# A lane shuffle, merged stack loads, held-back and column-tiled projections in the opening of an attention kernel

## The reference

```python
q, k, v = (x @ W + b for W, b in ((Wq, bq), (Wk, bk), (Wv, bv)))   # split in 16 heads of 16
q = q * cos + rotate_half_interleaved(q) * sin                      # pairs (-x1, x0)
k = k * cos + rotate_half_interleaved(k) * sin
x = layernorm(x + softmax(q @ k.T / sqrt(16)) @ v)
x_prev = x shifted by one token (zero first)
xr, xk = mu_r * x + (1 - mu_r) * x_prev, mu_k * x + (1 - mu_k) * x_prev
out = layernorm(x + sigmoid(xr @ W_r.T) * (relu(xk @ W_k.T) ** 2 @ W_v.T))
```

## Time and profile before

| | |
|---|---|
| time, median of 3 runs | 1582.94 us (1581.42 to 1584.07) |
| profiled execution, its own time | 1584.12 us |
| its span, first to last instruction | 1582.3 us |
| TensorE, VectorE, ScalarE, GpSimd busy | 98%, 85%, 72%, 21% |
| mean granted TensorE clock | 0.993 |

### The profile page before, as it was taken

How to read it: one execution, slowest core, us unless ns; L and a number is a source line. 1 busy time by engine, 2 the same in 40 slices (tenths; PEclk the granted TensorE clock), 3 DMA queues, 4 the chain that set the end, 5 groups by cost and what they waited for, 6 DMA issues and landing times. The chain is left out here.

```text
span 1582.3 us, 47773 instructions
## 1 busy us (share of the span) xinstructions
PE 1545.5 (98%) x21184; PEld 765.5 (48%) x21184; DVE 1345.3 (85%) x1398; ACT 1139.0 (72%) x2187; POOL 335.3 (21%) x327
## 2 busy tenths in 40 slices
PE   5999999999999999999999999999999999999997
PEld 3343445555445544455445444544444455443574
DVE  3447999999999999999999999999999999996577
ACT  3225777777777777777777777777777777778442
POOL 2330322112221322132213221121210000001165
PEclk9999999999999999999999999999999999999999
DMA  6625211121101111121112111211101111000012
GB/s 230 182 73 174 76 22 22 22 76 19 18 15 45 48 22 22 22 75 22 23 22 75 22 22 22 75 22 18 19 16 17 22 22 22 3 2 2 1 41 67
DMA packets 34735, 68.20 MB, mean 43 GB/s; under 512 B 9760, under 2 KB 19744, under 8 KB 32736
## 3 DMA queue, kind: packets, MB, share of 16 engines
q1 hardware_dynamic: 32560, 62.03, 16.0%
q10 hardware_dynamic: 1968, 3.12, 0.5%
HBM read 26.97 MB, written 11.53 MB: 24 GB/s over the span
## 5 line engine op out<-in xcount | busy, mean ns | idle before, releaser
L931 DVE TENSOR_REDUCE tile_max<-ring_ps 128x1 f32<-128x1024 f32 x1024 | 1204.2, 1216 | 164.6 <-PE ring_ps L446 163.5
L696 ACT ACTIVATE probs<-score_ps 128x512 f32<-128x512 f32 x2048 | 1059.6, 603 | 270.6 <-PE score_ps L543 270.1
L446 PE MATMUL ring_ps<-k_stack,q_stack 96*32 96x512 bf16 x8192 | 838.9, 381 | 11.0 <-DMA q_stack<-rope 10.1
L543 PE MATMUL score_ps<-q_stack,k_stack 99*32 99x512 bf16 x8192 | 841.7, 381 | 4.0 <-ACT probs L696 2.9
L479 PE MATMUL pv_ps<-probs,v_aug 128*32 128x512 f32 x4096 | 541.5, 592 | 0.0
L543 PEld LDWEIGHTS score_ps<-q_stack,k_stack 99*32 99x32 bf16 x8192 | 258.8, 96 | 311.7 <-ACT probs L696 146.8
L446 PEld LDWEIGHTS ring_ps<-k_stack,q_stack 96*32 96x32 bf16 x8192 | 253.5, 96 | 309.0 <-DVE tile_max L931 120.5
L479 PEld LDWEIGHTS pv_ps<-probs,v_aug 128*32 128x32 f32 x4096 | 146.7, 111 | 82.7 <-ACT probs L696 1.6
L773 POOL TENSOR_TENSOR neg_cuts<-neg_max,zeros 128x16 bf16<-128x16 f32 x32 | 7.0, 220 | 740.5 <-DVE neg_max L918 740.5
L766 POOL TENSOR_TENSOR v_aug<-v_all,b_v_s 128x256 f32<-128x256 f32 x32 | 23.3, 730 | 281.5 <-PE pv_ps L479 256.1
L425 PE MATMUL score_ps<-xz,w_qk_s 128*128 128x512 f32 x96 | 50.8, 657 | 6.4 <-DMA b_qk_s<-b_qk 6.4
(11 more groups left out here) (73 smaller groups left out, 544.6 us busy)
## 6 DMA issues: line engine op xcount, KB each, us to landing
q_stack<-rope SPq DMA_DIRECT2D x186, 64.0 KB, 2.4
k_stack<-rope SPq DMA_DIRECT2D x186, 64.0 KB, 2.4
qk_raw<-probs SPq DMA_DIRECT2D x28, 256.0 KB, 2.5
rope<-qk_raw SPq DMA_DIRECT2D x7, 1024.0 KB, 4.8
rope<-qk_raw SPq DMA_DIRECT2D x14, 512.0 KB, 6.9
xz<-x_ch SPq DMA_DIRECT2D x8, 512.0 KB, 6.7
xz<-x_tok SPq DMA_DIRECT2D x2, 2048.0 KB, 12.9
out<-xz SPq DMA_DIRECT2D x8, 512.0 KB, 2.9
```

What stands on the lines that cost most here:

```text
L446: mm = pe.matmul(ring_ps[k % 2][g:g + VCOLS, c * TOK:(c + 1) * TOK], q_stack[0:ROWS, buf, qt * P + g:qt * P + g + VCOLS], k_stack[0:ROWS, ...
L543: mm = pe.matmul(score_ps[n % SCORE_BANKS][g:g + VCOLS, :], k_stack[0:ROWS_M, h % STACKS, kt * P + g:kt * P + g + VCOLS], queries[:, j], s ...
L696: act.activation(probs[:, kt % 2, j, :], score_ps[n % SCORE_BANKS][:, :], ACT.Exp, scale=SCALE).then_inc(exps_done, 1)
L931: dve.reduce_max(tile_max[:, h % 2, unit // 2, unit % 2:unit % 2 + 1], slot[:, :], AX.X)\
```

## The change

- Quad 0 is taken out of PSUM by VectorE instead of ScalarE, in blocks of 512 columns: `stream_shuffle` exchanges neighbouring partitions, `scalar_tensor_tensor` adds the bias and multiplies by cosine or sine (`turn_block`). The swap DMAs go; the bias table has a fifth column with the exchanged biases. All cuts of quad 0 go by blocks of 512 (`block_of(n)`).
- A head's stacks are loaded by six DMAs: a query part is repeated over its bands in one transfer, and key parts 0 to reps - 1 go together.
- The x blocks of batch 1 are issued after head 0's stack loads. SyncE issues two stack loads behind each store.
- Batch 1's values are projected last instead of after its first quad. Five projections are held back and follow later entries of `OPENING` (`HELD_BACK`).
- Each projection matmul with 128-wide weights becomes four with 32-wide weights, to four column groups.
- `evacuated` counts from projection 4 on, so all waits on it are lower by 4; the new semaphore `quad0_taken` frees the first four banks.

```diff
@@ -25,9 +25,9 @@
-BANDS = [(a, c) for a in range(PARTS) for c in range(PARTS - a)]
-LOADS = 2 * len(BANDS)
-ROWS = len(BANDS) * HEAD_DIM
+BAND_GROUPS = [(a, PARTS - a) for a in range(PARTS)]
+LOADS = 2 * PARTS
+ROWS = sum(reps for _, reps in BAND_GROUPS) * HEAD_DIM
@@ -60,9 +60,11 @@
         yield from (("qk", first, n) for n in range(BLOCKS))
-        yield from (("v", b, n) for n in range(TILES // 2))
-        for g in range(first + 1, first + QUADS // BATCH):
-            yield from (("qk", g, n) for n in range(BLOCKS))
+        if b == 0:
+            yield from (("v", b, n) for n in range(TILES // 2))
+        yield from (("qk", g, n) for g in range(first + 1, first + QUADS // BATCH) for n in range(BLOCKS))
+        if b > 0:
+            yield from (("v", b, n) for n in range(TILES // 2))
@@ -89,6 +91,7 @@
+HELD_BACK = {("max", 0, MAX_UNITS - 1): 1, ("max", 1, 1): 1, ("neg", 0, 0): 1, ("max", 1, 2): 1, ("max", 1, 3): 1}
@@ -295,25 +302,21 @@
-            def swap(n):
-
-                sp.wait_ge(evacuated, n + 1)
-                t = slice(n * TOK, (n + 1) * TOK)
-                for e in range(2):
-                    sp.dma_start(swapped[e::2, t], raw[1 - e::2, t]).then_inc(swap_in[n // 2], DMA)
-
             def load_part(h, part, t):
 
                 buf, side, row = h % STACKS, h // QUAD % 2, h % QUAD * HEAD_DIM
-                for band, (a, c) in enumerate(BANDS):
-                    rows = slice(band * HEAD_DIM, (band + 1) * HEAD_DIM)
+                q = cuts[row:row + HEAD_DIM, side, :, t]
+                k = cuts[QUAD_ROWS + row:QUAD_ROWS + row + HEAD_DIM, side, :, t]
+                first = 0
+                for a, reps in BAND_GROUPS:
+                    rows = slice(first * HEAD_DIM, (first + reps) * HEAD_DIM)
+                    first += reps
                     if a == part:
-                        sp.dma_start(q_stack[rows, buf, t], cuts[row:row + HEAD_DIM, side, a, t])\
+                        sp.dma_start(q_stack[rows, buf, t], q[:, a:a + 1, :].broadcast_to([HEAD_DIM, reps, t.stop - t.start]))\
                             .then_inc(stack_in[buf], DMA)
                         yield
-                    if c == part:
-                        sp.dma_start(k_stack[rows, buf, t], cuts[QUAD_ROWS + row:QUAD_ROWS + row + HEAD_DIM, side, c, t])\
-                            .then_inc(stack_in[buf], DMA)
+                    if reps - 1 == part:
+                        sp.dma_start(k_stack[rows, buf, t], k[:, 0:reps, :]).then_inc(stack_in[buf], DMA)
                         yield
@@ -352,29 +355,23 @@
             for n in range(BLOCKS):
                 load_x(n)
-            swap(0)
-            swap(1)
-            load_x(BLOCKS)
-            load_x(BLOCKS + 1)
-            swap(2)
-            swap(3)
-            load_x(BLOCKS + 2)
-            load_x(BLOCKS + 3)
             for i in range(2):
                 for part, signal in enumerate((high_ready, mid_ready, low_ready)):
-                    sp.wait_ge(signal, i + 1)
+                    sp.wait_ge(signal, 2 * (i + 1))
                     for _ in load_part(0, part, half_of(i)):
                         pass
+            for n in range(BLOCKS, A_GROUPS):
+                load_x(n)
...
-                    for _ in range(3):
+                    for _ in range(2):
                         next(others, None)
@@ -409,7 +409,10 @@
-                after(pe, evacuated, n - len(proj_ps) + 1)
+                if n >= 2 * len(proj_ps):
+                    pe.wait_ge(evacuated, n - len(proj_ps) - BLOCKS + 1)
+                elif n >= len(proj_ps):
+                    pe.wait_ge(quad0_taken, n - len(proj_ps) + 1)
@@ -422,8 +422,9 @@
                     for c in range(CHUNKS):
-                        mm = pe.matmul(bank[:, :], w_qk_s[:, c, m:m + P], x_s[:, b, c, t:t + TOK],
-                                       start=c == 0, stop=c == CHUNKS - 1)
+                        for r in range(0, P, VCOLS):
+                            mm = pe.matmul(bank[r:r + VCOLS, :], w_qk_s[:, c, m + r:m + r + VCOLS],
+                                           x_s[:, b, c, t:t + TOK], start=c == 0, stop=c == CHUNKS - 1)
@@ -431,8 +432,10 @@
                         for c in range(CHUNKS):
-                            mm = pe.matmul(bank[:, k * DIM:(k + 1) * DIM], x_s[:, a, c, t:t + P], w_v_s[:, c, :],
-                                           start=c == 0, stop=c == CHUNKS - 1, skip_group_check=True)
+                            for r in range(0, P, VCOLS):
+                                mm = pe.matmul(bank[r:r + VCOLS, k * DIM:(k + 1) * DIM],
+                                               x_s[:, a, c, t + r:t + r + VCOLS], w_v_s[:, c, :],
+                                               start=c == 0, stop=c == CHUNKS - 1, skip_group_check=True)
@@ -573,10 +576,11 @@
-                if n < len(WORK):
+                if op in HELD_BACK or n + sum(HELD_BACK.values()) < len(WORK):
                     project(n)
                     n += 1
@@ -652,33 +656,35 @@
+            cut_high(0)
+            cut_high(1)
+            cut_mid(0)
+            take(BLOCKS)
+            cut_high(2)
+            cut_mid(1)
+            take(BLOCKS + 1)
+            cut_high(3)
+            cut_mid(2)
+            take(BLOCKS + 2)
+            cut_mid(3)
+            for n in range(BLOCKS + 3, len(WORK)):
                 take(n)
@@ -879,36 +885,48 @@
-            def turn_half(i):
-
-                t = half_of(i)
-                dve.wait_ge(tables_in[i], 2 * DMA)
-                dve.wait_ge(swap_in[i], 4 * DMA)
-                dve.wait_ge(evacuated, 2 * (i + 1))
-                dve.tensor_tensor(raw[:, t], raw[:, t], cos_s[:, t], ALU.mult)
-                dve.tensor_tensor(swapped[:, t], swapped[:, t], sin_s[:, t], ALU.mult).then_inc(products, 1)
-                dve.wait_ge(products, i + 1)
+            def turn_block(n):
+
+                t, bank = block_of(n), proj_ps[n]
+                dve.wait_ge(projected, n + 1)
+                dve.stream_shuffle(swapped[:, t], bank[:, :], [lane ^ 1 for lane in range(32)]).then_inc(swap_ready, 1)
+                if n == 0:
+                    dve.wait_ge(w_first_in, 2 * DMA)
+                dve.wait_ge(tables_in[n // 2], 2 * DMA)
+                dve.scalar_tensor_tensor(raw[:, t], bank[:, :], b_qk_s[:, 0:1], cos_s[:, t], ALU.add, ALU.mult)\
+                    .then_inc(quad0_taken, 1)
+                dve.wait_ge(swap_ready, n + 1)
+                dve.scalar_tensor_tensor(swapped[:, t], swapped[:, t], b_qk_s[:, QUADS // BATCH:], sin_s[:, t],
+                                         ALU.add, ALU.mult).then_inc(products, 1)
+                dve.wait_ge(quad0_taken, n + 1)
+                dve.wait_ge(products, n + 1)
                 dve.tensor_tensor(raw[:, t], raw[:, t], swapped[:, t], ALU.add).then_inc(rot_ready, 1)
...
-            turn_half(0)
+            turn_block(0)
+            turn_block(1)
             cut_rest(0)
-            turn_half(1)
+            turn_block(2)
+            cut_rest(1)
             cut_low(0)
-            cut_rest(1)
             cut_low(1)
+            turn_block(3)
+            cut_rest(2)
+            cut_rest(3)
+            cut_low(2)
+            cut_low(3)
```

More of the change, by code:

```diff
@@ L146, in build @@
         w_v_s = sb("w_v_s", [P, CHUNKS, DIM])
-        b_qk_s = sb("b_qk_s", [P, QUADS // BATCH])
+        b_qk_s = sb("b_qk_s", [P, QUADS // BATCH + 1])
         b_v_s = sb("b_v_s", [P, DIM])
@@ L217, in build @@
         stage_out = [sem(f"stage_out{i}") for i in range(STAGES)]
-        swap_in = [sem(f"swap_in{i}") for i in range(2)]
+        quad0_taken = sem("quad0_taken")
+        swap_ready = sem("swap_ready")
         raw_in = sem("raw_in")
@@ L280, in half_of, with block_of @@
             return slice(i * HALF, (i + 1) * HALF)
+        def block_of(n):
+            return slice(n * TOK, (n + 1) * TOK)
         def z_tile(tile):
@@ L326, in store_raw @@
                 s = STORED[g, t]
-                sp.wait_ge(evacuated, n + 1)
+                sp.wait_ge(evacuated, n - BLOCKS + 1)
                 sp.dma_start(raw_d[g, :, t * TOK:(t + 1) * TOK], stage[:, s % STAGES, :])\
@@ L336, in load_raw @@
                 if g == 1:
-                    sp.wait_ge(low_ready, 2)
+                    sp.wait_ge(low_ready, BLOCKS)
                 else:
@@ L376, in _ @@
             load_neg(0)
-            sp.wait_ge(evacuated, len(WORK))
+            sp.wait_ge(evacuated, len(WORK) - BLOCKS)
             for b in range(BATCH):
@@ L575, in _ @@
                     pass
-                if n < len(WORK):
+                if op in HELD_BACK or n + sum(HELD_BACK.values()) < len(WORK):
                     project(n)
                     n += 1
-            pe.wait_ge(evacuated, len(WORK))
+            assert n == len(WORK)
+            pe.wait_ge(evacuated, len(WORK) - BLOCKS)
             for h in range(ALL_HEADS):
@@ L654, in take, with cut_high, cut_mid @@
```

(49 more changed lines are left out.)

## The result

| | before | changed |
|---|---|---|
| median | 1583.12 us (1581.42 to 1584.07, 4 runs) | 1558.83 us (1558.47 to 1560.27, 4 runs) |
| ratio, 95% interval | | 0.9847 [0.9832, 0.9863] |
| profiled execution, span | 1584.12, 1582.3 | 1558.66, 1556.9 |

A forecast was written before the change was run, and what follows sets the result against it. TensorE, busy for all 42.0 of 42 us, was taken to bound the attention, so only its start moves: 8.4 + 16.2 + 0.2 = 24.8 us off the 1582.94 median gives 1558.1, range 1553 to 1570.

The forecast's parts named there:

- First maximum, 8.4 us: Opening: TensorE's first maximum begins at 32.2 us instead of 40.6, 8.4 us earlier.
- the two paths: Opening, before the first maximum: stack loads complete at 31.1 us, TensorE's projections 7 to 11 end at 31.6.
- Turn and stretch, 16.2 us: First maximum to first score: turns of 2.155 us instead of 2.46, stretch 78.7 instead of 94.9, 16.2 less.
- First scores, 0.2 us: First score to first probabilities-by-values product: 5.2 us instead of 5.40, held by VectorE's reading, 0.2 less.
- Attention and epilogue unchanged: After the way into the attention: nothing that runs there is touched, so times stay equal to the end.
- The sum: Whole kernel: 8.4 + 16.2 + 0.2 = 24.8 us saved, giving 1558.1; own range 1556 to 1561, chance 0.46.
- Rival A: Turns stay at 2.46 us if the bf16 to f32 change costs the 0.31: 11.2 us kept, 1569.3; chance 0.14.
- F: Projections: 107 ns is the floor of an f32 pair, value projections take 3.44 us, time 1580; chance 0.03.
- C: Projections: narrow tiles' weight loads stay exposed, 110 ns each, 58 us in the turns, time 1616; chance 0.03.
- the estimate from the 60 cycles a matmul: Projections: 12 or 24 added pairs at 25 ns cost 0.3 or 0.6 us each; sum 13 us smaller in turns.
- D: Opening: slow shuffle or late transfers put the first maximum at 34 to 36, 1560 to 1562; with B 0.20.
- B: Clock falls in the 2.8 us gap or first scores, costing 2 to 4 us: 1560 to 1562; with D 0.20.

The follow-up runs named there:

- the last kernel: The changed kernel with the gap filled (projections 4 to 7 in the idle ring banks, 13 before the first maximum) and a sixth projection held back: 1557.24 us, ratio 0.9837.

## Why the prediction was right, point by point

*First maximum, 8.4 us: right, 8.40.* That it is met so closely is partly luck: the two paths were worked out to end at 31.1 and 31.6, 32.2 was chosen above both, and they end at 31.8 (the last load, 29.48 + 2.3) and 32.24; the second profile has 32.75. The last low cut was forecast to end at 27.8 and ends at 27.97; the shuffle takes 0.73 us for the 0.70 taken from the transpose's row. One step in it was wrong, in the path of the loads: I let two issues follow the last cut, but SyncE was still busy with the mid part's, so the last load goes out at 29.48, 1.5 us behind the cut, instead of 0.7. The last load is also not a 96 KB one but the 32 KB of the low query part. It cost nothing, since TensorE's own projections end at 32.24, and that was one of the two paths. The experiments separate them: with twelve loads the stacks come last (3.06 us of waiting), and in the last kernel, with the gap filled, TensorE is ready first and waits 0.97 us for the stack load until 31.76. The two paths of the changed kernel end within half a microsecond.

*Turn and stretch, 16.2 us: right, 16.4.* Turns of 2.15 were forecast as 2.155. The chain of the maxima's DMA ran as worked out: the last maximum of head 0 is at T = 99.02, the DMA is issued at T + 5.4 (forecast T + 5.8) and the first score comes at T + 11.8 (T + 11.9). Whole-width projections bring back 11.0 us, so the tiles carry two thirds of the stretch; the rest is the clock at its start and the wait at its end.

*First scores, 0.2 us: 0.3.* VectorE's backlog holds TensorE back, as the ring unit at 111.83 and the sixth held-back projection show.

*Attention and epilogue unchanged: right.* 1441.0 against 1441.3 us.

*The sum.* 24.8 us was worked out, 25.5 lie between the two profiled executions and 24.3 between the medians. A second set of runs of the changed kernel has a median 1.1 us higher (1559.89), beside a kernel before at 1584.20: again 24.3.

*Rival A* (the turn stays at 2.46 because bf16 and f32 alternate) fell: the same data types make 2.15 us with four column groups and 2.41 with two. *F and C* (a floor or an exposed load for each narrow f32 pair) fell with the value turn of 2.16 us; in F's sum the 8.5 should be 8.75 (23.15 + 5 x 3.44 - 31.6), which changes nothing in the forecast. So did the estimate from the 60 cycles a matmul (Trainium skill, "TensorEngine Tiling (Array Packing)", Instruction Overhead): 24 added pairs cost nothing that the turn shows. Eight whole-width pairs fill the 1.72 us, 215 ns each, and 32 narrow ones of the same 256 columns fit in the same time only if four run side by side. *D* (late transfers) fell: 96 KB loads landed in 2.6 to 2.8 us in the changed kernel's two profiles, and SyncE's issues for head 0 have a median of 0.6, though one took 1.25 (26.29). *B*, the clock, is half right. It doesn't fall in the changed kernel's two profiles, but in two of its siblings with the same opening it does, and from TensorE's resuming to the first maximum it then takes 1.4 and 1.7 us more: not the 2 to 4 forecast, but what the prediction gave for one projection at the low clock, 1.7. The sum had no reason why the clock should hold in the gap; that it did in both profiles of the changed kernel is luck as far as is known.

*What each part is worth.* Each part taken out alone costs, against 1558.8: tiles 10.8 us, rotary part 6.9, values last 5.3 (of which 1.4 are the clock in its gap), six loads 3.4, holding back 1.1. They add up to 27.5, 3 more than the whole, but that excess isn't shown to mean anything: the changed kernel's second median is 1559.9, against which each is 1.1 less, holding back nothing, and the sum 22.1. What is seen in the traces is that the rotary part and the loads each also keep the clock up, and that the order's figure has the accident in the gap in it.

## What to carry to other kernels

Where tiled and whole-array matmuls alternate, try the whole-array ones in the tile width of their neighbours: here the streaming time was equal, and 0.31 us a round trip went away; another width kept nearly all of the loss. A queue that issues in order delays a small, urgent transfer by whatever its neighbours wait for, so order the producers such that the last ones need no store. When an opening gets shorter, look for who now waits without being named in the change: here TensorE waited for four PSUM banks while the ring's, another four blocks of 512 columns, were idle, and filling that gap took about 2 us more (1.8 between the medians the first time, on different chips, 2.6 side by side).

## What the runs showed of the hardware that was not expected

- A column tiling of 64 beside one of 32 costs nearly as much as the whole array beside 32: 2.41 and 2.46 us a turn against 2.15.
- 32 f32 load and matmul pairs of 128x32 weights and 256 columns run in the 1.72 us between two ring units, 54 ns a pair, as the bf16 pairs do.
- The same opening code, with a stop of TensorE between 20.4 and 24.1 us, kept the granted clock at 1.00 in some executions and had 0.50 in 24 to 26 in others. The stops are 2.44 and 2.68 us in the changed kernel's two profiles, without a fall, and 2.79 us in the two with one (values early, no projections held back); whether length decides is not shown by four profiles.
- The granted clock can fall far into the kernel, with no edit near it: 0.94 and 0.95 in 1470 to 1500 with the tiles alone and the 64-wide projections, 0.96 in 1430 to 1470 with the gap filled; from the first product to the end it then takes 1442.8 to 1443.0 us instead of 1441.0.
- A transfer that reads 16 rows of SBUF three times over into 48 rows lands nearly like one of the same size that reads 48 different rows (96 KB in 2.7 and 2.6 us).
